# Second attention of a two-layer transformer: TensorE's order written out step by step instead of planned

## The reference, cut to what matters

```python
c_kv = x @ W_kv_down
k_rope = _rotary_apply(c_kv @ W_k_rope, cos, sin)
k = (c_kv @ W_k_up).reshape(Bb, Tt, NH, HD)          # 16 heads of 8
v = (c_kv @ W_v_up).reshape(Bb, Tt, NH, HD)
q = (x @ W_q).reshape(Bb, Tt, NH, HD)
q_rope = _rotary_apply(x @ W_q_rope, cos, sin)       # 32 columns, shared by the heads
scores = (einsum(q, k) + einsum(q_rope, k_rope)[:, None]) / scale
scores = where(causal, -inf, scores)                 # 1024 x 1024 for each batch and head
w = softmax(scores)
attn = einsum(w, v); return attn @ W_o
```

## Time and profile before

| | |
|---|---|
| median of 3 runs | 1463.19 us (1461.65 to 1468.33) |
| the profiled execution | 1461.15 us, of which the span of the engines is 1459.4 us |
| the second attention in the span | about 878 to 1204.8 us |
| TensorE busy over the span | 94% |
| VectorE, GpSimd, ScalarE busy | 67%, 59%, 55% |

### The profile page before, as it was taken

How to read it: one execution, slowest core, us unless ns; L and a number is a source line. 1 busy time by engine, 2 the same in 40 slices (tenths; PEclk the granted TensorE clock), 3 DMA queues, 4 the chain that set the end, 5 groups by cost and what they waited for, 6 DMA issues and landing times. The chain is left out here.

```text
span 1459.4 us, 18725 instructions
## 1 busy us (share of the span) xinstructions
PE 1364.8 (94%) x6370; PEld 787.1 (54%) x6370; DVE 972.7 (67%) x1673; ACT 808.9 (55%) x1236; POOL 863.4 (59%) x683
## 2 busy tenths in 40 slices
PE   6799999999999999999988876999999988999998
PEld 5354445545554555455466534454445445778776
DVE  5767676777777776766557578676666625566665
ACT  4344445445444545354464452666776666787776
POOL 0397888898888888778444314555655233344443
PEclk9699999999999999999999987999999998999999
DMA  3110111111111111000140006111111107000000
GB/s 108 34 44 16 59 60 59 59 45 59 59 37 39 59 60 45 1 15 27 27 150 1 1 1 101 16 31 30 31 22 24 30 1 276 1 1 9 8 8 8
DMA packets 32586, 60.59 MB, mean 42 GB/s; under 512 B 9499, under 2 KB 17084, under 8 KB 32348
## 3 DMA queue, kind: packets, MB, share of 16 engines
q1 hardware_dynamic: 32492, 59.40, 14.7%
HBM read 35.13 MB, written 13.89 MB: 34 GB/s over the span
## 5 line engine op out<-in xcount | busy, mean ns | idle before, releaser
L631 POOL TENSOR_TENSOR psum_k<-psum_k,prob 128x1024 f32<-128x1024 f32 x184 | 460.0, 2532 | 107.1 <-ACT prob L683 106.8
L683 ACT ACTIVATE prob<-pair 128x1024 f32<-128x1024 f32 x256 | 246.5, 1026 | 335.7 <-PE pair L943 335.7
L742 DVE TENSOR_REDUCE mx<-pair 128x2 f32<-128x1024 f32 x256 | 297.2, 1216 | 43.3 <-PE pair L869 41.5
L915 PE MATMUL pv<-prob,c_all 128*64 128x512 f32 x1024 | 250.8, 606 | 0.9 <-ACT plain L651 0.9
L1946 DVE CUSTOM_DVE_ANT_0 l_banks<-l_banks,causal 128x128 f32<-128x128 f32 (+7 forms) x256 | 189.4, 783 | 74.6 <-PE l_banks L1984 73.5
L1854 ACT ACTIVATE l_prob<-l_banks 128x1024 f32<-128x1024 f32 (+7 forms) x256 | 155.1, 654 | 111.1 <-PE l_banks L2003 110.4
L942 PE MATMUL pair<-qq,ak 128*128 128x512 f32 x512 | 208.2, 407 | 1.9 <-DMA q<-mrow 0.9
L943 PE MATMUL pair<-q,kb 128*128 128x512 f32 x512 | 201.0, 393 | 0.0
L2162 POOL TENSOR_TENSOR silu_rest_t<-silu_t,silu_lead_t 128x512 fp32r<-128x512 f32 x74 | 96.2, 1300 | 143.2 <-ACT silu_lead_t L2359 143.2
L1908 POOL TENSOR_SCALAR_AFFINE_SELECT l_prob<-l_prob 128x128 f32<-128x128 f32 x256 | 71.9, 292 | 146.9 <-ACT l_prob L1854 145.3
L942 PEld LDWEIGHTS pair<-qq,ak 128*128 128x128 f32 x512 | 96.2, 188 | 65.4 <-issue 25.6
(11 more groups left out here) (320 smaller groups left out, 2282.9 us busy)
## 6 DMA issues: line engine op xcount, KB each, us to landing
plain<-scratch_sums SPq DMA_DIRECT2D x32, 256.0 KB
whole<-in_experts SPq DMA_DIRECT2D x12, 512.0 KB, 5.0
scratch_lead<-rounded SPq DMA_DIRECT2D x12, 512.0 KB, 2.6
scratch_rest<-rounded SPq DMA_DIRECT2D x12, 512.0 KB, 3.9
w_lead_t<-scratch_lead SPq DMA_DIRECT2D x9, 512.0 KB, 6.4
w_rest_t<-scratch_rest SPq DMA_DIRECT2D x9, 512.0 KB, 7.3
l_kk<-rounded SPq DMA_DIRECT2D x16, 256.0 KB, 4.2
l_qq<-rounded SPq DMA_DIRECT2D x16, 256.0 KB, 5.4
```

The source lines that it names most:

```text
L631: nc.gpsimd.tensor_tensor(total[:, h, :], total[:, h, :], prob[kt % 4][:, h, :], ALU.add).then_inc(summed, 1)
L683: nc.scalar.activation(prob[kt % 4][:, :, ts(j, BLK)], buffer("ST", at)[:, :, :], ACT.Exp, scale=D0 ** -0.5).then_inc(exp_done, 1)
L742: nc.vector.reduce_max(mx[:, x % 2, :, x // 2], buf[:, :, :], AX.X).then_inc(read, 1)
L915: ins = nc.tensor.matmul(pv[D0 * h:D0 * (h + 1), ts(j, BLK)], m.c_all[:, TT * (s // PAIRS) + kt, :], prob[kt % 4][:, h, ts(j, BLK)], start ...
```

## The change

`plan1()` no longer chooses. The order is four strings, one letter per item, each letter taking the next item of its stream: one for what stands ahead of step 0, one for step 0, one that is repeated for steps 1 to 5, one for steps 6 and 7. The pass through the order only assigns banks, still the bank or pair free soonest, by new durations. The items, their matmuls, their readers and their waits stay as they are; the order of every engine's part follows the list.

```diff
 def pass_time(width):
-    return max(0.2, 0.24 * width / BLK)
+    return max(0.062, 0.231 * width / BLK)
...
     if kind == "PV":
         lo, hi = q_pieces(item[2])[item[3]]
-        return 0.15 + 0.95 * (hi - lo) / BLK
+        return 0.04 + 0.86 * (hi - lo) / BLK
...
     if kind == "ST":
-        return 0.17 + 0.85 * (T - P * item[2]) / T
+        return 0.12 + 0.86 * (T - P * item[2]) / T
...
+START1 = ("kkkkkkssssssskssssssssskssssssssssssssss")
+FIRST1 = ("TTTsTTTsTVTssVsksTVsTTVsTkssTVTTksssVTTsTsTTkssVVTssTVTTTsTsssTTVTsTTsTTVs")
+STEP1 = ("TTTsTVskkssVsTsTsVTsTTsksTVTTtksssVTTsVTsTVTsTsVTsTVTsTTTVsTsssTTTVTsTsTTVs")
+LAST1 = ("TTVsTsTTTsVTsTVsTTVTsTVsTssVsTTVssTTTsTVsTsVssTTsTTsVTTTTsVTTTVTTTTTVtTTTVTVTTTVTVTTVTTVTTTTVVTT"
+         "TTVTTTTVTTTTVVtt")
...
+def sequence1():
+    streams = [iter(stream) for stream in streams1()]
+    return [next(streams["TVskt".index(kind)]) for kind in START1 + FIRST1 + STEP1 * (STEPS1 - 3) + LAST1]
...
 def plan1():
-    queues = [list(s) for s in streams1()]
...
-    while any(queues):
-        found = []
...
-        _, _, start, q, banks = min(found)
-        item = q.pop(0)
+    order, place, before = sequence1(), {}, {}
+    for item in order:
...
+        if want == 1:
+            banks = (min(range(BANKS), key=lambda x: (free[x], -free[x ^ 1])),)
+        else:
+            banks = min([(x, x + 1) for x in range(0, BANKS, 2)], key=lambda x: max(free[x[0]], free[x[1]]))[:want]
```

More of the change, by code:

```diff
@@ L1585, in pe_time @@
         lo, hi = q_pieces(item[2])[item[3]]
-        return 0.15 + 0.95 * (hi - lo) / BLK
+        return 0.04 + 0.86 * (hi - lo) / BLK
     if kind == "e":
-        return 2 * pass_time(s_width(item[2]))
+        return 2 * max(0.11, pass_time(s_width(item[2])))
     if kind == "s":
         return pass_time(BLK) + pass_time(s_width(item[2]) - BLK)
-    return {"k": 1.0, "q": 1.0, "m": 0.2, "t": 0.9}[kind]
+    return {"k": 0.86, "q": 0.86, "m": 0.2, "t": 0.9}[kind]
 def read_time(item):
@@ L1597, in read_time @@
     if kind == "ST":
-        return 0.17 + 0.85 * (T - P * item[2]) / T
+        return 0.12 + 0.86 * (T - P * item[2]) / T
     if kind in "es":
-        return (2 if kind == "e" else 1) * (0.16 + s_width(item[2]) / 960)
-    return {"k": 1.4, "q": 1.4, "m": 0.3, "t": 0.8, "PV": 0.0}[kind]
+        return (2 if kind == "e" else 1) * (0.14 + s_width(item[2]) / 1000)
+    return {"k": 1.35, "q": 1.35, "m": 0.3, "t": 0.75, "PV": 0.0}[kind]
 def banks_of(item):
@@ L1631, in rope_copy_behind @@
     return (k, j, g) if k in ROPE_FILLS and k >= 2 else None
+START1 = ("kkkkkkssssssskssssssssskssssssssssssssss")
+FIRST1 = ("TTTsTTTsTVTssVsksTVsTTVsTkssTVTTksssVTTsTsTTkssVVTssTVTTTsTsssTTVsTTsTTVs")
+STEP1 = ("TTTsTVskkssVsTsTsVTsTTsksTVTTtksssVTTsVTsTVTsTsVTsTVTsTTTVsTsssTTTVTsTsTTVs")
[4 more added lines that the diff above has]
+    return [next(streams["TVskt".index(kind)]) for kind in START1 + FIRST1 + STEP1 * (STEPS1 - 3) + LAST1]
@@ L1634, in plan1 @@
 def plan1():
-    queues = [list(s) for s in streams1()]
-    order, place, before = [], {}, {}
+    order, place, before = sequence1(), {}, {}
+    assert len(order) == len(set(order)) == sum(len(stream) for stream in streams1())
     free, holder = [0.0] * BANKS, [None] * BANKS
-    done, clock = {}, {"PE": 0.0, "ACT": 0.0, "DVE": 0.0, "POOL": 0.0}
-    def ready(item):
+    done, pe, act, dve, pool = {}, 0.0, 0.0, 0.0, 0.0
+    for item in order:
         kind, n = item[0], item[1]
-        if kind == "ST":
[L1645 to L1652, removed]
-        elif kind == "m":
[L1654 to L1666, removed]
-    while any(queues):
-        found = []
[L1670 to L1678, removed]
-        _, _, start, q, banks = min(found)
-        item = q.pop(0)
[L1681 to L1710, removed]
@@ new lines, in plan1 @@
+        start, want = pe, banks_of(item)
+        if kind == "ST" and item[2] == 0:
+            start = max(start, done[("row", n, item[3] // 2)])
+        elif kind == "PV":
+            start = max(start, done[("masked", n, item[2])], done.get(("ut", n - 1), 0.0))
+        elif kind in "es":
+            start = max([start] + [done[("loaded", n, int(kind == "s"), x)] for x in "kq"])
+        elif kind == "m":
+            start = max([start] + [done[("s", n, TT - 1, 2 * item[2] + h)] for h in range(2)])
+        elif kind == "t":
+            start = max(start, done[("ut", n)])
@@ new lines, in plan1 @@
+        if want == 1:
+            banks = (min(range(BANKS), key=lambda x: (free[x], -free[x ^ 1])),)
+        else:
+            banks = min([(x, x + 1) for x in range(0, BANKS, 2)], key=lambda x: max(free[x[0]], free[x[1]]))[:want]
+        place[item] = banks[0] if banks else None
+        before[item] = sorted({holder[x] for x in banks if holder[x] is not None})
+        pe = max([start] + [free[x] + TURN for x in banks]) + pe_time(item)
+        if kind == "PV":
+            done[("pv", n, item[2])] = pe
+            if item[2] == TT - 1:
+                act = max(act, pe + TURN, done.get(("t", n - 1), 0.0)) + 1.0
+                done[("ut", n)] = act
+            continue
@@ new lines, in plan1 @@
+        if kind in ("ST", "k", "q"):
+            back = TT * n + item[2] - 2
+            late = done[("pv", back // TT, back % TT)] if kind == "ST" and back >= 0 else 0.0
+            end = act = max(act, pe + TURN, late) + read_time(item)
+        else:
+            end = dve = max(dve, pe + TURN) + read_time(item)
+        done[item] = end
+        for x in banks:
+            free[x], holder[x] = end, item
+        if kind == "ST":
+            act += 0.5 * (rope_copy_behind(item) is not None)
+            pool = max(pool, end) + 0.27
+            done[("masked", n, item[2])] = pool
+            if item[3] == 3 and item[2] % TPB == TPB - 1:
+                done[("freed", n, item[2] // TPB)] = pe + TURN
+                if n + 2 in ROPE_FILLS:
+                    pool = max(pool, pe + TURN) + 2.3
+        elif kind in "kq":
+            if n:
+                made = pool = max([pool, end] + [done[("loaded", n - 1, item[2], x)] for x in "kq"]) + 2.85
+            else:
+                made = dve = max(dve, end) + 0.8
+            done[("loaded", n, item[2], kind)] = max(made, done.get(("freed", n - 2, item[2]), 0.0)) + 5.0
+        elif kind == "m":
+            done[("row", n, item[2])] = end + 2.2
```

## The result

The changed kernel takes 1450.22 us in the median of 5 runs (1449.14 to 1455.09), the kernel before 1463.87 (1461.65 to 1468.33). The ratio is 0.9911, with a 95% interval of 0.9892 to 0.9929: 0.7 to 1.1% faster. The profiled execution took 1449.32, with a span of 1447.6 where it was 1459.4.

The account below looks back on a forecast made before the run. The stage was taken as bound by the turn of three bank pairs. Steps 0 to 5 -3.6, start -0.7, end -0.2 sum to -4.5 us: 1458.7 against the median of 1463.19, range 1446 to 1469.

Parts of the forecast that it names:

- the full pay: Rival: the listed order removes all 2.6 us of unexplained waits a step, 1446.7; chance 0.23 together with half pay.
- the walk: Hand walk of both orders of step 5 through three bank pairs: 35.4 us each, so 0.0 between them.
- Only waits change: Whole change: no instruction added or removed, readers' durations stay, so every term is a difference of waits.
- Steps 1 to 5, -0.6 each: Second attention's repeated steps: a gain of 0.6 us each, with bounds of 2.6 gained and 1.3 lost.
- The start, -0.7, and step 0, -0.6: Before and in step 0: s, m and six e ahead of T0a gain 0.7 (0 to 1.5); step 0 gains 0.6.
- one rival: At the start, longer waits for DVE before T0a halve the clock, costing 5 us: 1464; chance 0.05.
- Steps 6 and 7, -2.0, and the end, +1.8: m moved to step 6 saves 2.0 us; t behind the last V delays ACT's last copy, costing 1.8.
- The banks, nothing: Bank assignment by the new durations: no gain or loss taken.
- The heads' load: Steps 1 to 5: cover shrinks from 2.6 to 0.6 us; rival, PE stalls, 1472; chance 0.13 together with the front.
- The front with rotary copies: Rival: fronts of steps 3 and 4 pay 1.5 us more, others 0.6, 1468; chance 0.13 together with heads' load.
- The gain in full: Rival: each step's unexplained 2.6 us vanish, 1446.7; half of it, 1.3 a step, 1454.5; chance of either 0.23.
- The signs named beforehand: Trace signs: steps of 37 to 38 us, no DMA wait before first s, ACT's last copy over 2 after last V.

Follow-up runs that it names:

- both halves: Two runs: the order of before with banks assigned by the changed kernel's durations, 1463.19 us; the changed kernel's list with banks by the old durations, 1448.21 us.
- the old rest: The changed kernel with the planner's order of before behind block 2 in steps 1 to 5, the new order up to there: 1460.23 us, ratio 0.9983.

## Why the prediction was right, and what in it was off

The direction, the place and the range held: 1450.2 lies between 1446 and 1469. The forecast itself, 1458.7, named a gain too small to be told from none. The gain was three times as large by the medians and two and a half times in the stage (11.3 for 4.5), and the chance given to a gain that shows was 0.35. So that the time fell inside the range is owed more to the range's width, which took in nearly the full pay, than to the walk. By its steps:

- **Only waits change.** Right: the readers' busy times are the same, and the old list with the new banks is the old time (1.0007).
- **Steps 1 to 5, -0.6 each.** This is the term that was mis-sized. It is -1.2 to -2.5 a step, in all -8.2 where -3.0 was said. In step 5 the walk of the new list was 0.4 short in each of the three parts (13.0, 12.3, 10.2; the trace has 13.4, 12.7, 10.6). The walk of the old list was 0.4, 1.0 and 1.2 short. It had the new list's last part 0.9 longer, where the trace has the two alike: for the old list it found 0.2 of waits there, and the trace has 1.4. So of the 2.6 that the walk left unexplained, half (1.3) stays in the new order and half was the old order's own. A quarter of it was too small a share. In steps 2 and 3 the old list had another 0.5 in the last part (11.0), which I didn't walk. The walk's own sums are loose by as much: 13.0 + 12.3 + 10.2 is 35.5 and not 35.4, and the new list's work adds up to 31.5 where the same items in the old one make 31.2.
- **The start, -0.7, and step 0, -0.6.** Together -2.6. Counted from the first projection, the exponential of T0c comes 1.5 earlier, which is the far end given to the start's term, and the rest of step 0 is 1.1 shorter. The other eleven profiles with the new start and the new step 0 need 77.5 to 79.0 to step 1 and the other one with the old start 81.3, so the gain is that of the start's order. The clock did not fall as one rival had it: the granted clock from the first projection to step 1 is 0.87, where it was 0.82. How much of the 2.6 is the clock's, no run separates.
- **Steps 6 and 7, -2.0, and the end, +1.8.** Measured -3.2 and +2.8. Right in mechanism, and nearly in size: from T0a of step 7 to its block 2 it takes 8.6 where it took 10.5, -1.9. The other 1.3 lie in step 6 (0.4) and in the later blocks of step 7 (0.9), which had no term. Of the end's 1.0 too little, 0.9 is the lower clock in the last transposes (1.94 for 1.09), which the sum had not. Where the transposes of this end take 1.06, the way to the next stage is 5.7, +1.9.
- **The banks, nothing.** Right, shown by both halves.
- **The heads' load.** Its cover was worked out at 0.6. It is 0.5 in the changed kernel's step 5, did not run out, and does so when the s items stand 1.7 earlier. In steps 3 and 4 the first s comes only 6.8 after the step's start, so the cover there is 1.5. The rival was real and did not come to pass.
- **The front with rotary copies.** This rival did not come to pass either: steps 3 and 4 take 1.2 more than their neighbours, where before they took 1.3 and 1.8 more than step 5. The new order doesn't pay more for the copies than the old one did.
- **The gain in full.** What happened lies between its half and its whole: a step gained 1.65 on average, where half of the way is 1.3 and the whole 2.6.
- **The signs named beforehand.** All held but one, and that by little: steps 1, 2 and 5 take 36.7, under the 37 to 38 that were named. No weights of an s item wait for DMA in steps 1 to 5, and ACT's last copy starts 2.4 after the last V.

What makes blocks 2 and 3 faster is shown only in part. Of 1.7, the spread of the values gives 0.4 and the s items ahead of block 3 give 0.4, each alone. Whether the remaining 0.9 is the place of t, k and q between them, or that the parts help each other, stays open; moving q alone in the old rest made it worse.

## What to carry to other kernels

When several engines follow one list, an item costs not its own time but that of what it makes the others wait for. Ask of each item that waits on another engine's queue what stands before its releaser *there*: three scores moved ahead in TensorE's order put a copy three exponentials later in ScalarE's, and only the transposes' late place kept that off the path. Such a list is a fit as a whole: each of the seven edits tried inside the new step cost 0.4 to 4.9 us a step, also the old front, which the hand walk had called the better one, and they are judged by the part of the step in the trace sooner than by the total. And where a hand walk explains only part of a stage's waits in the old order, the rest may be the gain: here half of it was, in the step that was walked.

## What the runs showed of the hardware that was not expected

In steps 1 to 5 TensorE stood still for up to 1.1 us at a time (1.08 in the kernel before, 1.10 in the run with t at the front), and the granted clock stayed at 1.00. Longer waits in steps 3 and 4 were followed by half clock in the next items: 2.59 in front of the transposes (transposes 1.94 in place of 1.09, the granted clock of step 4's front 0.83), and 1.75 in front of the s items, in the run with s ahead of k (first projection 1.91 in place of 1.02, the front 0.90).

The length of the wait alone doesn't tell what follows. At the end of the attention a wait of 2.10 was followed by transposes of 1.06 or 1.07 in five profiles, 1.20 in one, 1.56 or 1.57 in two and 1.94 in two. A wait of 1.22 was followed by 1.06 or 1.07 in three profiles, and by 1.94 in the profile of the old list with the new banks:

```profile
1204.08 1.94 PE L2031 MATMUL l_banks<-ident,plain 128*128 128x128 f32 x8 [1.22 <-ACT plain L1863]
```
